# An audio tower on one core: the token stage written out per pair, with its own order for the last rounds, and the first expert tile fetched at the end of the first block

## Time and profile before

| | |
|---|---|
| median of 3 runs | 1067.77 us (1062.13 to 1068.28) |
| the profiled execution | 1060.41 us, span 1058.5 us |
| TensorE busy | 909.3 us, 86% |
| VectorE | 801.6 us, 76% |
| ScalarE | 608.9 us, 58% |
| GpSimd | 552.6 us, 52% |
| token stage, to the end of the table | 0 to 358.5 us |
| no engine busy | 358.5 to 368.8 us |
| expert stage, from the first up-matmul | 384.6 to 1058.5 us |

### The profile page before, as it was taken

One profiled execution on the slowest core, in us unless ns is written; L12 is line 12 of the kernel. 1 busy time (PEld: TensorE's weight loads), 2 busy tenths in 40 slices (PEclk: granted clock), 3 DMA queues, 4 the chain that ended last, 5 costly groups with the idle time before them and its releaser, 6 DMA issues. The chain is left out here.

```text
span 1058.5 us, 19059 instructions
## 1 busy us (share of the span) xinstructions
PE 909.3 (86%) x5742; PEld 769.5 (73%) x5742; DVE 801.6 (76%) x2058; ACT 608.9 (58%) x1166; POOL 552.6 (52%) x461
## 2 busy tenths in 40 slices
PE   4788887888754059999999999999999999999994
PEld 3456565555533049988988998998998998999893
DVE  1799999999993357787787787777777778778761
ACT  2798888888871035564554564555556545556441
POOL 0104665646464353575575566467557457457424
PEclk9999999999985569999999999999999999999997
DMA  8342534433111064565564466457447456556423
GB/s 264 120 149 91 169 102 139 129 120 89 37 54 45 16 220 176 125 146 141 164 161 139 121 199 157 114 141 207 126 127 209 129 122 163 180 125 146 125 26 40
DMA packets 71671, 138.97 MB, mean 131 GB/s; under 512 B 10925, under 2 KB 62766, under 8 KB 67658
## 3 DMA queue, kind: packets, MB, share of 16 engines
q0 software_dynamic: 31136, 98.34, 35.2%
q1 hardware_dynamic: 40490, 40.08, 12.3%
HBM read 110.52 MB, written 27.86 MB: 131 GB/s over the span
## 5 line engine op out<-in xcount | busy, mean ns | idle before, releaser
L1055 ACT ACTIVATE hid<-hp,b 128x512 f32<-128x512 f32 (+1 forms) x248 | 158.6, 639 | 303.0 <-PE hp L1090 297.8
L1102 PE MATMUL acc<-whi,hhi 128*128 128x256 f32 x880 | 246.0, 280 | 0.0
L1102 PE MATMUL acc<-whi,hlo 128*128 128x256 f32 x880 | 245.9, 279 | 0.0
L1102 PE MATMUL acc<-wlo,hhi 128*128 128x256 f32 x880 | 245.3, 279 | 0.0
L1186 DVE CAST hhi<-hid 128x512 fp32r<-128x512 f32 (+1 forms) x248 | 107.2, 432 | 148.1 <-ACT hid L1055 147.4
L1017 POOL DMA_INDIRECT out_rows<-yout,dest x110 | 179.8, 1634 | 63.9 <-issue 45.8
L1090 PE MATMUL hp<-xhi,whi 128*128 128x512 f32 (+1 forms) x496 | 187.6, 378 | 10.0 <-DVE xlo L1133 7.7
L341 POOL DMA_INDIRECT expert_lists<-tid,slots x96 | 134.0, 1396 | 113.1 <-DVE cand L736 56.3
L1090 PE MATMUL hp<-xlo,whi 128*128 128x512 f32 (+1 forms) x496 | 183.8, 371 | 0.0
L1090 PE MATMUL hp<-xhi,wlo 128*128 128x512 f32 (+1 forms) x496 | 183.6, 370 | 0.0
L1031 ACT ACTIVATE whi<-raw 128x512 fp32r<-128x512 f32 x248 | 154.3, 624 | 41.3 <-DMA raw<-in_ew,idx 41.3
(11 more groups left out here) (185 smaller groups left out, 1442.2 us busy)
## 6 DMA issues: line engine op xcount, KB each, us to landing
xin<-in_x SPq DMA_DIRECT2D x32, 512.0 KB
xin<-in_x SPq DMA_DIRECT2D x32, 256.0 KB
token_rows<-xs SPq DMA_DIRECT2D x16, 388.5 KB, 3.9
out_rows<-h SPq DMA_DIRECT2D x16, 384.0 KB, 2.6
xg<-token_rows,tid POOLq DMA_INDIRECT x110, 2.9
out_rows<-yout,dest POOLq DMA_INDIRECT x110, 4.1
expert_lists<-tid,slots POOLq DMA_INDIRECT x96, 5.3
out_rows<-zrow SPq DMA_DIRECT2D x1, 512.0 KB
```

What stands on the lines that cost most here:

```text
L1055: act.activation(hid[:, c % 2, 0:j.r * P], hp[c % 2][:, 0:j.r * P], ACT.Relu, bias=b1[:, j.s, c:c + 1]).then_inc(hid_done, 1)
L1102: last = pe.matmul(acc_of(j, r), h_[:, c % 4, r * P:(r + 1) * P], w_[:, j.s, at:at + C], start=c == 0 and n == 0 and r % 2 == 0, stop=c == ...
```

## The change

- `rounds` no longer loops: every engine has rounds 0 to 15 written out (`body`), with plain numbers in waits and addresses, and rounds 16 to 19 from a second function (`drain`) with an order of its own. The operations become small named functions. The order in `body` is the old one; semaphore increments that only marked the end of a wait are gone.
- In `drain`, VectorE has pair p4's placing first, all of p3's choosing together ahead of the residual sum of p2, and the statistics of p2 together. TensorE, ScalarE and GpSimd keep their order.
- `tok` and its step are gone: `tid` for all 16 pairs comes from one iota and one copy at the start. `slots` has 16 buffers, `xs` three instead of two. GpSimd's list writes wait for `placing` alone.
- `lnd`, `lner` and `lsum` are written in place of `den`, `er` and `den`. `raw` and `xg` of the expert stage lie over `h`, in `Tables`, with `idx`, the tile's `tid` and their semaphores.
- After the table, VectorE copies the indices of tiles 0 and 1 in the first block. GpSimd then fetches tile 0's weights, waits for all list writes, fetches its token list, waits for the stored rows and fetches its rows, all in the first block; `first` of the second block begins with tile 1, token list ahead of weights.
- The first block ends without GpSimd's drain, and SyncE no longer waits for the list writes.

The diff, cut to its core:

```diff
 class Pair:
-    def __init__(self, g, s):
-        self.g, self.s = g, s
+    def __init__(self, q):
+        self.q, self.s = q, q % 2
     def at(self, per_pair, more=0):
-        return self.g * (2 * per_pair) + (per_pair * self.s + more)
+        return self.q * per_pair + more
...
+class Fetch:
+    def weights(self, j):
+        t = self.tables
+        self.pool.indirect_dma_start(t.raw[:, j.s, :], None, self.ew, bass.IndirectOffsetOnAxis(t.idx[:, j.i, 0:1], 0)).then_inc(t.w_in[j.s], 16)
+    def tokens(self, j):
+        t = self.tables
+        self.pool.indirect_dma_start(t.tid[:, j.s, 0:j.r], None, self.groups[j.r],
+                                     bass.IndirectOffsetOnAxis(t.idx[:, j.i, 1:2], 0)).then_inc(t.tid_in[j.s], 16)
+    def rows(self, j):
+        t = self.tables
+        for r in range(j.r):
+            self.pool.indirect_dma_start(t.xg[:, j.s, r, :], None, self.rows_of,
+                                         bass.IndirectOffsetOnAxis(t.tid[:, j.s, r:r + 1], 0)).then_inc(t.x_in[j.s], 16)
...
-def rounds(eng, body, until=PAIRS):
+def rounds(body, drain):
     def pairs(i):
-        return [Pair((i - lag) // 2, (i - lag) % 2) if 0 <= i - lag < PAIRS else None for lag in range(STEPS)]
-    ahead = STEPS // 2 + 1
-    for i in range(2 * ahead):
+        return [Pair(i - lag) if 0 <= i - lag < PAIRS else None for lag in range(STEPS)]
+    for i in range(PAIRS):
         body(*pairs(i))
-    with eng.Fori(1, until // 2 - ahead + 1) as n:
-        for s in range(2):
-            body(*(Pair(n + (ahead - 1 - (lag + 1 - s) // 2), (s - lag) % 2) for lag in range(STEPS)))
-    for i in range(until, PAIRS + STEPS - 1):
-        body(*pairs(i))
+    for i in range(PAIRS, PAIRS + STEPS - 1):
+        drain(*pairs(i)[1:])
...
-        tok_i, tok = sb("tok_i", [P, 3], I32), sb("tok", [P, 3])
+        tok_i, tid = sb("tok_i", [P, PAIRS, 3], I32), sb("tid", [P, PAIRS, 3], U32)
...
-        den, lnd, lner = sb("den", [P, SEQ, T]), sb("lnd", [P, SEQ, T]), sb("lner", [P, SEQ, T])
-        lsum, inv = sb("lsum", [P, SEQ, T]), sb("inv", [P, SEQ, T])
+        den, inv = sb("den", [P, SEQ, T]), sb("inv", [P, SEQ, T])
+        lnd, lner, lsum = den, er, den
...
-        block = ctx.enter_context(nc.Block())
+        block = ctx.enter_context(nc.Block(no_gpsimd_drain=True))
...
+            def scatter(q):
+                pool.wait_ge(placing, q.at(N_PLACE, N_PLACE))
+                for c in range(6):
+                    pool.indirect_dma_start(lists, bass.IndirectOffsetOnAxis(slots[:, q.q, c:c + 1], 0),
+                                            tid[:, q.q, c % 3:c % 3 + 1], None).then_inc(listed[q.s], 16)
...
+            fetch, t0 = Fetch(pool, tables, ew, rows, lists), Tile(0, 0)
+            pool.wait_ge(tables.idx_ready, 1)
+            fetch.weights(t0)
+            for s in range(2):
+                pool.wait_ge(listed[s], 96 * (PAIRS // 2))
+            fetch.tokens(t0)
+            pool.wait_ge(all_rows, 1)
+            pool.wait_ge(tables.tid_in[0], 16)
+            fetch.rows(t0)
...
+            def drain(p1, p2, p3, p4):
+                if p4:
+                    places(p4)
+                    new_ends(p4)
+                if p3:
+                    shift_2(p3)
+                if p2:
+                    weighted(p2)
+                if p4:
+                    second_places(p4)
+                    gate_sum(p4)
+                if p2:
+                    weighted_sum(p2)
+                if p4:
+                    first_places(p4)
+                    first_gate(p4)
+                if p2:
+                    numerator(p2)
+                if p4:
+                    second_gate(p4)
+                    first_slots(p4)
+                    second_slots(p4)
+                if p2:
+                    output(p2)
+                if p1:
+                    running_max(p1)
+                    difference(p1)
+                    sigmoid_divisor(p1)
+                if p3:
+                    lg_in(p3)
...
+                    selected(p3)
+                if p2:
+                    residual(p2)
+                    for t in range(3):
+                        statistic_2(p2, t)
+                    for t in range(3):
+                        mean_2(p2, t)
+                if p1:
+                    weights_sum(p1)
+                    divisor(p1)
+                    value_now(p1)
+                    log_sum(p1)
...
             def first():
-                pool.wait_ge(idx_ready, 1)
-                gather_tid(T0)
-                gather_w(T0)
-                gather_x(T0)
                 pool.wait_ge(idx_ready, 2)
-                gather_tid(T0.nxt())
+                fetch.tokens(T0.nxt())
+                fetch.weights(T0.nxt())
                 gather_b2(T0)
-                gather_w(T0.nxt())
                 gather_x(T0.nxt())
```

More of the change, by code:

```diff
@@ new lines, in decays, with now, log_sigmoid @@
+                act.activation(es[:, :, :, 1:TP], dist[:, :, :, :], ACT.Exp, scale=-1.0).then_inc(exps, 1)
+            def now(q):
+                for k in range(HC):
+                    a = slice(2 * k, 2 * k + 2)
+                    act.activation(ey[:, a, :], dl[:, a, :], ACT.Exp, bias=u[:, k:k + 1]).then_inc(exps, 1)
+            def log_sigmoid(q):
+                act.wait_ge(state, q.at(N_STATE, 1))
+                act.activation(lner[:, :, :], er[:, :, :], ACT.Ln).then_inc(inv_ready, 1)
@@ L439, in _ @@
+            rounds(body, drain)
         @block.tensor
@@ new lines, in value_now, with log_sum @@
+            def value_now(q):
+                dve.wait_ge(kr_taken, q.at(4, 4))
+                dve.wait_ge(exps, q.at(N_EXP, N_EXP))
+                dve.wait_ge(state, q.at(N_STATE))
+                dve.scalar_tensor_tensor(out=t2[:, :, :], in0=ey[:, :, :], scalar=CAP, in1=v[:, q.s, :, 1:TP],
+                                         op0=ALU.min, op1=ALU.mult).then_inc(state, 1)
+            def log_sum(q):
+                dve.wait_ge(inv_ready, q.at(N_INV, 2))
+                dve.tensor_tensor(flat(lsum[:, :, :]), flat(lnd[:, :, :]), flat(lner[:, :, :]), ALU.add).then_inc(state, 1)
@@ new lines, in selected, with places, new_ends @@
+            def selected(q):
+                chosen(q, 14)
+                dve.tensor_tensor(sel[:, :, :], oh1[:, :, :], oh2[:, :, :], ALU.add).then_inc(choice, 1)
+            def places(q):
+                dve.wait_ge(rank_done, q.at(1, 1))
+                placed(q, 0)
+                dve.tensor_tensor(place[:, :, :], rank_ps.rearrange("p (t e) -> p t e", e=E), over_t(ends[:, :]), ALU.add).then_inc(placing, 1)
+            def new_ends(q):
+                placed(q, 1)
+                dve.tensor_tensor(ends[:, :], tot_ps, ends[:, :], ALU.add).then_inc(placing, 1)
@@ L608, in body, with second_slots @@
+            def second_slots(q):
+                placed(q, 3)
+                with nc.allow_low_precision("whole numbers"):
+                    dve.tensor_reduce(slots[:, q.q, 3:6], pl2[:, :, :], AX.X, ALU.add).then_inc(placing, 1)
             def body(p0, p1, p2, p3, p4):
                 if p4:
-                    dve.wait_ge(rank_done, p4.at(1, 1))
-                    placed(p4, 0)
-                    dve.tensor_tensor(place[:, :, :], rank_ps.rearrange("p (t e) -> p t e", e=E), over_t(ends[:, :]), ALU.add).then_inc(placing, 1)
+                    places(p4)
@@ L745, in body @@
[L745 to L752 removed]
+                    second_number(p3)
@@ L970, in gather_x @@
                 end_of_waits()
[L971 to L973 removed]
+                fetch.rows(j)
             def gather_b2(j):
@@ L997, in body @@
                     end_of_waits()
-                    gather_w(a)
-                    gather_tid(a)
+                    fetch.weights(a)
+                    fetch.tokens(a)
                 if p.exists():
```

751 lines of the change are left out of this document (441 added, 310 removed).

## The result

| | before | after |
|---|---|---|
| median | 1066.61 us (1062.13 to 1068.28) | 1035.97 us (1034.05 to 1036.54, 4 runs) |
| profiled execution | 1060.41 us, span 1058.5 | 1034.05 us, span 1032.3 |

The ratio of the medians is 0.972, 95% interval 0.968 to 0.975. Between the two traces lie 26.4 us where 18.5 were forecast; that is 7.9 of the miss of 13. The other 5 come from the profiled run of before, which lay 7 us under the median that the forecast started from, while that of after lies 2 us under its own.

What follows compares the result with a forecast made beforehand. VectorE was held to pace the looped rounds, waits the tail, with an idle gap between blocks. Rounds -8.3 plus tail and gap -10.1 make 18.4, rounded to 18.5: 1049 us from the median 1067.77, range 1038 to 1061.

Steps and rivals of the forecast that it cites:

- the change leaves its rounds alone: Expert stage, bound by TensorE: its rounds were held to be untouched by the change, so no gain was counted there.
- the expert stage as long as before, 674 us plus 1 to 2: Sign: first up-matmul to the end stays 674 us plus 1 to 2; wrong if it changes by over 3 us.
- Part 3: Gap between the blocks: fetching tile 0 early and dropping the drain bring the first up-matmul 11.4 us earlier, tail included.
- This now lies beside the list writes: Gap: tile 0's weights, issued at 351.8, land 8.6 us later, at 360.4, while list writes are still landing.
- The weights have 3 us of theirs left, so I take 360.6: Gap: token list, issued at 357.3 behind the weights, lands at 360.6, at worst 364.9.
- GpSimd comes to the barrier at 365.5 only, and everybody waits for it: End of block one: all engines wait for GpSimd's row gathers; barrier 2.5 us, block two begins at 368.0.
- Tile 1's weights: Start of block two: fetched 3.5 us before the first up-matmul (before 4.5); ScalarE waits 2 to 3 us, TensorE loses 1.3.
- Rival 2: The gap moves instead of closing: tail and gap give only 4 us, time 1055.5; chance 0.12.
- Part 1: Rounds 0 to 15 written out: 17.7 us a round instead of 18.5 in the loop, -8.3 us in all.
- Rival 1: Rounds do not shrink, held by TensorE's half clock and ScalarE's chain: only 10 us come, 1057.5; chance 0.15.
- rival 3: Written-out rounds starve engines of instructions, 3.9 us a stop; one stop a round gives 1088; chance 0.05.
- Part 2: Tail, rounds 16 to 19: new VectorE order and more buffers start pair 15's last list write 7.5 us earlier.

Runs made afterwards that it cites:

- f1: Changed kernel with 32 unused bytes a partition before `whi` and 32 behind `wlo`; one run, full tiles 23.38 to 23.45 us, list write to first up-matmul 26.8 us.
- g1 to h2: Six versions of f3, buffers behind `wlo` moved by 32, 128, 192, 448, 64 or 480 bytes; one run each, full tiles 23.35 to 23.48 us.
- h3: Kernel before with 384 unused bytes a partition between `wlo` and `b1`, nothing else; ratio to before 0.993, full tiles 22.95 us.
- e0: Kernel before and changed kernel, both unchanged, run again on another chip; ratio 0.975, list write to first up-matmul 28.5 and 26.8 us.
- f2: Kernel before with 32 unused bytes a partition before `whi`, moving all these buffers together; ratio to before 1.000, full tiles 23.38 us.
- i2: f3 once more, on one chip with i1; ratio to before 0.971, median 1031.57 us, list write to first up-matmul 24.0 us.
- i1: Changed kernel unchanged, once more, beside i2; ratio to before 0.975, median 1035.60 us, list write to first up-matmul 27.9 us.
- f3: Changed kernel with tile 0's token list issued ahead of its weights, both after the lists landed; ratio to before 0.971, list write to first up-matmul 24.6 us.
- f4: Changed kernel with GpSimd's drain put back into the barrier after the token stage; one run, list write to first up-matmul 34.6 us.
- e1: Kernel before with rounds 6 to 15 written out instead of looped, nothing else; ratio to before 0.995, rounds 5 to 15 176.6 us.
- e0_after_again: Changed kernel, unchanged, run again on another chip; ratio to before 0.975, rounds 5 to 15 175.4 us.
- e0_before_again: Kernel before, unchanged, run again on the same chip as e0_after_again; ratio 1, rounds 5 to 15 183.4 us.

## Why the prediction was wrong

**The step that failed: "the change leaves its rounds alone", and "the expert stage as long as before, 674 us plus 1 to 2".** It was 9.2 us shorter. The forecast had listed `raw` and `xg` over `h`, and asked of it only whether it adds a wait. It adds none. But it takes 41 KB a partition from in front of and between the expert stage's buffers, and these come to lie at other distances from each other. TensorE is busy for 96% of the stage, so its pace is the stage's: 0.42 us less at fifteen distances between full tiles, 0.21 behind each of seven half-size ones, 0.8 in the remaining distances and 0.7 behind the last transposes make the 9.2. f1, g1 to h2 and h3 show it from both sides. The forecast said it would be wrong if this stage changed by more than 3 us; the sentence did its work, the reason it gave, that the code and the instructions are the same, did not carry.

**Part 3 failed in its sum, and two of its reasons with it**: forecast -3.9 us between the last list write and the first up-matmul, measured +0.1 in the first pair of traces, -1.7 in e0, and -3.3 between f1 and f2.
- "This now lies beside the list writes": it hardly does. The weights were issued 7 us before the lists landed, but only 0.48 of their 2.1 MB had started by 350.7, in packets of 1.3 to 7.4 us instead of 0.61. In i2, where they are issued behind the list writes' landing, the first ones take 0.8 to 1.7 us. From issue to landing the early weights needed 11.9 us in f1 and 13.0 in i1, where the median of all 31 is 8.7. I had put the token list behind the weights in this queue, but not the weights behind the list writes.
- "The weights have 3 us of theirs left, so I take 360.6": with four fifths of the weights' packets still to start, the token list needs its whole 7.5 us, as in every expert round. The end put at 364.9 was the right pricing (lists landed + 7.6); in the new kernel that is 349.57 + 7.5 = 357.07.
- "GpSimd comes to the barrier at 365.5 only, and everybody waits for it", 2.5 us: it didn't happen. ScalarE starts block two 1.4 us after the first of four row gathers; the second has started 0.13 us before, the last two are still to be issued. This error was in the kernel's favour. The first row gather came 18.5 us after the last list write where 12.4 had been forecast, the first up-matmul 28.9 instead of 25.0, so it hid some 2 of the 6 us. The block began 19.9 us after that write, forecast 19.8: the late rows and the barrier that waits for nobody cancelled there, which is luck. The forecast had this too among what would show it wrong, and also the first up-matmul "within 6 us of the block's start": it came after 9.1, as it waited for the rows.
- The lists landed 10.7 us after the last write's start, before 8.8; in f3, f4, i1 and i2 8.6 to 9.8. No run explains the spread.
- Tile 1's weights: ScalarE waits 0.76 us (forecast 2 to 3, before 1.50). They are issued 4.1 us before the first up-matmul (before 4.5), but landed 8.5 us after their issue instead of 9.65.

Rival 2, "the gap moves instead of closing", is what the gap did; its time (1055.5) missed because the other parts gave more.

**Part 1 was right in kind and 1 to 2 us too small.** 17.7 us a round was forecast, 17.47 measured, near the lower end. I took one round in three to meet the half clock; it was one in ten, for TensorE's first projections were slow enough to hold VectorE in the last round only. Rival 1, that the loop costs nothing, is refuted by e1. The 0.15 us a round for the token counter, its copy and the increments were too much: e1 still has them, and its undisturbed rounds take 17.39 us against 17.36 in e0_after_again. The other 1 us between the two runs lies in three rounds of e1 (17.72 to 17.74), each with 0.24 to 0.35 us more idle time at one operation. The rounds that were written out before too did not gain the 0.15 each either: 1 to 5 and 15 to 16 together took 87.6 us before and 88.5 after. No round shows a stop of 3 us, so rival 3 is out. The Trainium skill (Runtime: NRT & Kernel Launch, "Instruction fetch mechanics") has straight code fetched ahead and mostly hidden; eight of ten written-out rounds within 0.01 us of each other agree with it.

**Part 2 was right in each of its three stretches**, read from the two traces; no run isolates the new order. (Its terms as written add up to -7.7, the sum says 7.5.) From the scan of round 16 to the residual sum +2.0 us (forecast +1.5: 24.80 against 22.77); from there to pair 15's logits -2.5 (forecast -2.3); from there to the last list write -7.4 (forecast -6.9). The choice chain of round 16 runs at 0.21 us a link from 296.45 to 299.08, as priced. By the rule of the Trainium skill (VectorE: DVE Perf Modes, "The DRAIN you can't avoid"), a semaphore between chained operations costs nothing extra and the +1.5 would have fallen away. The trace doesn't agree: the links start 0.20 to 0.22 us apart, the operations beside others 0.07 to 0.10, and the residual sum came 2.0 us later.

## What to carry to other kernels

When a stage is bound by TensorE, any change that moves its buffers is a change of that stage, even if no instruction of it differs: compare a tile's length before and after first, and try the offset between the stationary and the moving buffers as a parameter of its own (32-byte steps here, up to 2% of a tile). An early issue is only worth what the transfers in flight let it move: ask what is issued ahead of a transfer in its queue and has not landed, and what small transfer somebody waits for stands behind it. Put the small one first.

## What was not expected of the hardware

- The same matmuls at the same granted clock (1.00 in every full tile compared) run 2% slower or faster by the distance of their two operands' buffers. Of the seven distances modulo 512 bytes that were tried, one (64) gave 22.96 us a tile, the others 23.35 to 23.48. That distances 0 and 256 give the same length to 0.01 us speaks for a period of 256; with one such pair that isn't shown. Why 64 is good, and whether single distances (`wlo` to `xhi`, `whi` to `hhi`) could be chosen better one by one, is open: all were moved together, and `hp<-xlo,whi` alone was faster at 0 and 256 than at 64.
- Half clock alone did not make the looped rounds long. Before, five of the nine had their first projections at full clock (1.55 or 1.56 us, at 127.30, 182.82, 219.25, 237.40 and 275.08) and took 18.23 to 18.95 us; in three of them (18.60, 18.85 and 18.95) VectorE waits 0.73 to 1.10 us for the output projection. In e0_before_again one such round took 17.76. A written-out one takes 17.37. What each looped round loses where was not followed further; the two lines are of the round that starts at 228.22 and takes 18.85:

```profile
233.05 0.96 DVE L690 TENSOR_TENSOR h<-wo_ps,h 128x768 f32<-128x768 f32 x1 [0.98 <-PE wo_ps L488]
...
237.40 1.56 PE L496 MATMUL kr_ps<-xnT,wk 128*128 128x384 f32 x4 [0.68 <-ACT xnT L430]
```

- A barrier without GpSimd's drain didn't wait for its indirect DMAs (block two began with two of four gathers unissued); with the drain and four gathers on the way it cost 7.8 us more, where before, with every list write landed, the whole wait was 3.9.
